# Last layer: the relative scores laid out with the heads innermost, and moved in two halves of 64 rows

## What is computed

```python
attn_scores = jnp.einsum('bhtd,bhsd->bhts', q, k)
rng = jnp.arange(Tx)
rel_pos = jnp.clip(rng[None, :] - rng[:, None], -MAX_REL, MAX_REL) + MAX_REL
rel_emb = rel_pos_emb[rel_pos]
rel_scores = jnp.einsum('bhtd,tsd->bhts', q, rel_emb)
attn = jax.nn.softmax((attn_scores + rel_scores) * scale, axis=-1)
out = jnp.einsum('bhts,bhsd->bhtd', attn, v)
```

## Time and profile before

| | |
|---|---|
| median of 3 runs | 1720.91 us (1717.68 to 1722.53) |
| the profiled execution | 1716.83 us, span 1715.1 us |
| last layer, first and last L707 | 1119.6 and 1656.7 us, 64 tiles |
| L707, one instruction | 1757 ns |
| DVE's wait for `relb` ahead of L707, whole run | 56.7 us |
| DMA share in 1300 to 1600 us | 0.85 |
| mean granted clock | 0.957 |

### The profile page before, as it was taken

How to read it: one execution, slowest core, us unless ns; L and a number is a source line. 1 busy time by engine, 2 the same in 40 slices (tenths; PEclk the granted TensorE clock), 3 DMA queues, 4 the chain that set the end, 5 groups by cost and what they waited for, 6 DMA issues and landing times. The chain is left out here.

```text
span 1715.1 us, 58930 instructions
## 1 busy us (share of the span) xinstructions
PE 1576.5 (92%) x18950; PEld 1439.4 (84%) x18950; DVE 1268.9 (74%) x2908; ACT 1124.7 (66%) x3086; POOL 806.8 (47%) x1457
## 2 busy tenths in 40 slices
PE   3999999999288999999999999679999999999987
PEld 2888888887278999999999999568888888888873
DVE  5899999997784555555555555378899889989876
ACT  2899999998193333433334333288899999999961
POOL 4576667663003222232322322356677776777620
PEclk9999999999598999999999999788999999999987
DMA  4122222222117988888889899286788888888844
GB/s 127 46 73 72 70 70 70 71 72 51 35 37 203 262 252 261 256 256 257 253 258 247 266 257 248 77 220 183 213 227 230 228 223 219 223 222 227 220 117 148
DMA packets 350388, 302.17 MB, mean 176 GB/s; under 512 B 44637, under 2 KB 315442, under 8 KB 350322
## 3 DMA queue, kind: packets, MB, share of 16 engines
q1 hardware_dynamic: 329984, 261.37, 54.5%
q0 software_dynamic: 16032, 37.51, 8.7%
q10 hardware_dynamic: 4306, 2.44, 0.6%
HBM read 208.17 MB, written 93.05 MB: 176 GB/s over the span
## 5 line engine op out<-in xcount | busy, mean ns | idle before, releaser
L1077 ACT ACTIVATE prob<-ps_s,b1s 128x256 f32<-128x256 f32 x426 | 178.8, 471 | 345.3 <-PE ps_s L1044 307.0
L972 POOL DMA_INDIRECT xs<-zn_d,idx x71 | 68.7, 968 | 366.5 <-PE ps_t L1008 364.9
L1044 PE MATMUL ps_s<-xhi,w1hi_c 128*128 128x256 f32 x852 | 236.2, 295 | 1.6 <-ACT xhi L1070 1.6
L1044 PE MATMUL ps_s<-xhi,w1lo_c 128*128 128x256 f32 x852 | 227.1, 284 | 0.0
L1019 PE MATMUL ps_v<-probT,prob 128*128 128x192 f32 x852 | 208.4, 326 | 0.0
L1019 PE MATMUL ps_k<-probT,prob 128*128 128x192 f32 x852 | 208.2, 326 | 0.0
L408 PE MATMUL ps_q<-xT,wqk_c 128*128 128x128 f32 x1536 | 202.8, 284 | 2.2 <-ACT xT L640 2.2
L408 PEld LDWEIGHTS ps_q<-xT,wqk_c 128*128 128x128 f32 x1536 | 194.4, 200 | 5.3 <-ACT xT L640 3.1
L619 ACT ACTIVATE kT<-ps_q,halves 128x128 f32<-128x128 f32 (+1 forms) x512 | 173.0, 366 | 4.9
L1044 PEld LDWEIGHTS ps_s<-xhi,w1hi_c 128*128 128x128 f32 x852 | 164.5, 193 | 2.0 <-ACT xhi L1070 2.0
L1044 PEld LDWEIGHTS ps_s<-xhi,w1lo_c 128*128 128x128 f32 x852 | 164.4, 193 | 0.0
(11 more groups left out here) (225 smaller groups left out, 4180.1 us busy)
## 6 DMA issues: line engine op xcount, KB each, us to landing
rel_d<-rpad SPq DMA_DIRECT2D x64, 864.0 KB
relb<-rel_d SPq DMA_DIRECT2D x64, 768.0 KB, 5.1
probT<-w2h SPq DMA_DIRECT2D x71, 576.0 KB
score<-w1h SPq DMA_DIRECT2D x71, 384.0 KB, 3.4
score<-w1h SPq DMA_DIRECT2D x142, 192.0 KB, 4.5
ys_d<-ys SPq DMA_DIRECT2D x71, 192.0 KB
tok<-b2h SPq DMA_DIRECT2D x71, 96.0 KB
posb<-pos_w SPq DMA_DIRECT2D x128, 48.0 KB, 2.6
```

Of the source, the lines that this page charges most:

```text
L972: pool.indirect_dma_start(xs[b][:, s, :], None, zn_d, bass.IndirectOffsetOnAxis(ap=ix[b][:], axis=0)).then_inc(x_ld[b], 16)
L1044: last = pe.matmul(dst, w, x, start=(k == 0), stop=(k == len(terms) - 1))
L1077: last = act.activation(hT[b][:, c, :], ps_s[:, j, (c % 2) * BLK:(c % 2) * BLK + BLK], ACT.Gelu, bias=b1s[b][:, c:c + 1])
```

## The change

The free dimension of `rpad`, `rel_d` and `relb` is turned from (head, column) to (column, head). So a row of `rel_d` is one contiguous piece, and so is what is stored and loaded of it. The shift of a row is now 12 elements. Store and load are cut in two, rows 0 to 63 and 64 to 127. Rows 0 to 63 need only the columns from 64 on (960 elements of 1728) in the store, and have non-zero values only for keys up to 79 (960 elements of 1536) in the load; the rest of `relb` is set to zero once, by POOL, before its first gathers. ACT reads PSUM in the new order, and DVE reads `relb` with a step of 12 elements from key to key.

```diff
-                        after(act, M[l]["rst"][b], 16 * st.pair("r"))
-                        src = ps_r_in.rearrange("p g (a j) -> p g a j", a=A)
-                        dst = rpad[b][:].rearrange("p (g a) j -> p g a j", g=G)
-                        act.activation(dst[:, :, :, 0:LPAD], src[:, :, :, 0:1].to_broadcast([128, G, A, LPAD]),
-                                       ACT.Copy)
-                        act.activation(dst[:, :, :, LPAD:LPAD + REL], src, ACT.Copy).then_inc(S["r_sb"], 1)
+                        after(act, M[l]["rst"][b], 32 * st.pair("r"))
+                        src = ps_r_in.rearrange("p g (a j) -> p j g a", a=A)
+                        dst = rpad[b][:].rearrange("p j (g a) -> p j g a", g=G)
+                        act.activation(dst[:, 0:LPAD], src[:, 0:1].to_broadcast([128, LPAD, G, A]), ACT.Copy)
+                        act.activation(dst[:, LPAD:LPAD + REL], src, ACT.Copy).then_inc(S["r_sb"], 1)
...
-                        dve.wait_ge(M_["rld"][b], 16 * (st.pair("s") + 1))
-                        dve.tensor_tensor(sc, psv, relb[b][:].rearrange("p (g a) k -> p g a k", g=G),
+                        dve.wait_ge(M_["rld"][b], 32 * (st.pair("s") + 1))
+                        dve.tensor_tensor(sc, psv, relb[b][:].rearrange("p k (g a) -> p g a k", g=G),
                                           ALU.add).then_inc(S["s_rd"], 1)
...
-        rpad = two("rpad", [128, H, LPAD + REL])
-        relb = two("relb", [128, H, B])
+        rpad = two("rpad", [128, LPAD + REL, H])
+        HALVES = [(0, B // 2), (B // 2, B)]
+        relb = two("relb", [128, B, H])
...
-                        heads = rel_d[b][:, 0:HEADW * H].rearrange("t (h c) -> t h c", h=H)
-                        sp.dma_start(heads[:, :, 0:LPAD + REL], rpad[b][:]).then_inc(M_["rst"][b], 16)
-
-                        sp.wait_ge(M_["rst"][b], 16 * (st.pair("r") + 1))
+                        for r0, r1 in HALVES:
+                            c = slice((B - r1) * H, (LPAD + REL) * H)
+                            sp.dma_start(rel_d[b][r0:r1, c], rpad[b][:].rearrange("p j h -> p (j h)")[r0:r1, c])\
+                                .then_inc(M_["rst"][b], 16)
+
+                        sp.wait_ge(M_["rst"][b], 32 * (st.pair("r") + 1))
...
-                        w = ROWW - 1
-                        src = rel_d[b].rearrange("t w -> (t w)")[B - 1:B - 1 + B * w].rearrange("(t w) -> t w", w=w)
-                        src = src[:, 0:HEADW * H].rearrange("t (h c) -> t h c", h=H)[:, :, 0:B]
-                        sp.dma_start(relb[b][:], src).then_inc(M_["rld"][b], 16)
+                        w = ROWW - H
+                        src = rel_d[b].rearrange("t w -> (t w)")[(B - 1) * H:(B - 1) * H + B * w]
+                        src = src.rearrange("(t w) -> t w", w=w)
+                        for r0, r1 in HALVES:
+                            c = slice(0, min(B, r1 + MAXREL) * H)
+                            sp.dma_start(relb[b][:].rearrange("p k h -> p (k h)")[r0:r1, c], src[r0:r1, c])\
+                                .then_inc(M_["rld"][b], 16)
...
             def _(pool):
+                for p in range(2):
+                    pool.memset(relb[p][0:B // 2, B // 2 + MAXREL:B, :], 0.0).then_inc(rel_zero, 1)
                 pool.wait_ge(E_["posi2"], 2)
```

More of the change, by code:

```diff
@@ L1339, in _ @@
             for p in range(2):
-                act.dma_start(rel_d[p][:, 0:HEADW * H].rearrange("t (h c) -> t h c", h=H)[:, :, LPAD + REL:2 * B - 1],
-                              zrow[:].rearrange("p (h c) -> p h c", h=H)).then_inc(rel_zero, 16)
+                act.dma_start(rel_d[p][:, (LPAD + REL) * H:(2 * B - 1) * H], zrow[:]).then_inc(rel_zero, 16)
             output_columns(act, 0)
@@ L1395, in tower @@
         E_ = {"posi2": sem("E_posi2")}
-        rpad = two("rpad", [128, H, LPAD + REL])
-        relb = two("relb", [128, H, B])
+        rpad = two("rpad", [128, LPAD + REL, H])
+        HALVES = [(0, B // 2), (B // 2, B)]
+        relb = two("relb", [128, B, H])
         def in_tiles(buf, width):
-            return buf[:].rearrange("p h s -> p (h s)")[:, 0:NT * width].rearrange("p (t n) -> p t n", n=width)
+            return buf[:].rearrange("p s h -> p (s h)")[:, 0:NT * width].rearrange("p (t n) -> p t n", n=width)
         fg, fr = in_tiles(relb[1], NODES), in_tiles(rpad[0], NODES)
@@ L1404, in tower @@
         prod = in_tiles(relb[0], LEAVES)
-        cT4 = [relb[0][:].rearrange("p h s -> p (h s)")[:, 1024 + 128 * p:1152 + 128 * p] for p in range(2)]
+        cT4 = [relb[0][:].rearrange("p s h -> p (s h)")[:, 1024 + 128 * p:1152 + 128 * p] for p in range(2)]
         fc = sb("fc", [128, NT, 32])
@@ L1419, in decode_pool @@
             if n == 67:
-                pool.wait_ge(M[1]["rst"][0], 16 * (NT // 2))
+                pool.wait_ge(M[1]["rst"][0], 32 * (NT // 2))
                 pool.memset(fr, 1.0).then_inc(F_["fr"], 1)
@@ L1528, in _ @@
                 S, M_ = L[1], M[1]
-                sp.wait_ge(rel_zero, 32)
+                sp.wait_ge(rel_zero, 34)
                 def body(st):
@@ L1535, in body @@
                         settle(sp, spare)
-                        after(sp, M_["rld"][b], 16 * st.pair("r"))
+                        after(sp, M_["rld"][b], 32 * st.pair("r"))
                         settle(sp, spare)
-                        heads = rel_d[b][:, 0:HEADW * H].rearrange("t (h c) -> t h c", h=H)
-                        sp.dma_start(heads[:, :, 0:LPAD + REL], rpad[b][:]).then_inc(M_["rst"][b], 16)
-                        sp.wait_ge(M_["rst"][b], 16 * (st.pair("r") + 1))
+                        for r0, r1 in HALVES:
[3 more added lines that the diff above has]
+                        sp.wait_ge(M_["rst"][b], 32 * (st.pair("r") + 1))
                         settle(sp, spare)
```

## The result

The changed kernel takes 1732.41 us (median of 7 runs, 1726.3 to 1736.29) against 1720.91 us of the kernel before (7 runs, 1717.07 to 1724.69), a ratio of 1.0065 with a 95% interval of 1.0048 to 1.0082: slower, by 11.5 us. The forecast was 1788 us. Direction and bound were right, the size was not: +67 us were forecast.

A forecast was written before the change was run, and what follows sets the result against it. The store-landing-load-store ring bounded the kernel at 8.33 us per tile; DVE would take over. At 9.5 us, 53 tiles add 62 us, early tiles 8, the start 0.5: 1788 us forecast, range 1730 to 1835.

The forecast's parts named there:

- The present bound: Steady tiles before the change: store, landing, load and next store set 8.33 us per tile, no engine does.
- the ring: SP's cycle of store, landing, load and next store of a tile, said to set 8.33 us per tile.
- DMA bytes and the shorter ring: Stores and loads: 1.33 MB for 1.67 in longer pieces, so the cycle falls to 6.1 to 7.2 us, below all engines.
- ACT reads PSUM freely: ACT, L631 and L633: reading PSUM in the new order costs nothing; upper bound 1.4 us more per tile.
- DVE, L707: Stepped read of `relb`: 3.35 us, 1.6 us more per tile, making DVE the bound at 9.14 us.
- PE waits, and its clock falls: PE at L490: about 1.4 us of waiting per tile brings clock falls, taking the tile from 9.14 to 9.5 us.
- The early tiles: The ten tiles ahead of the steady ones: half the DVE price each, +8 us.
- POOL's memsets: Two memsets ahead of the first gather, about 0.55 us each, half hidden: 0.5 us on the path, once.
- 1: Rival: DVE's step costs nothing and the shorter transfers pay, 7.85 us per tile, 1688 us; chance 0.18.
- 2: Rival: 64-row transfers move slower, deciding below some 245 GB/s; at 209 GB/s 9.2 us per tile, 1765 us; chance 0.04.
- 3: Rival: ACT's PSUM reads cost double, DVE's reads nothing; ACT needs 9.25 us per tile, 1765 us; chance 0.03.
- 4: Rival: half-size prices cancel the faster transfers, L707 at some 2.5 us, 1717 to 1726 us; chance 0.03.

The follow-up runs named there:

- e7_flat_whole: The changed kernel with one store and one load of all 128 rows, and DVE reading `relb` in the order in which it lies: 1684.11 us, ratio 0.9802.
- e3_whole: The changed kernel without the halves, one store and one load of all 128 rows a tile: 1719.41 us, ratio to before 1.0024.
- e12: The changed kernel with two stores and two loads a tile, each of all 128 rows and half of the columns: 1720.51 us, ratio 1.0014.
- e6: The kernel before, its layout and flat DVE read kept, with the changed kernel's halves and widths: 1722.25 us, ratio 1.0013.
- e9: A kernel of its own, timing stepped DVE additions, ScalarE copies, loads and stores one at a time; DVE's addition takes 1757 ns at step 1.
- e10: The changed kernel with an added DVE operation on 832 scratch elements ahead of L706 in each tile: 1761.51 us, ratio 1.0249.
- e8: The changed kernel with an added DVE operation on 416 scratch elements ahead of L706 in each tile: 1742.36 us, ratio 1.0126.
- e2: The kernel before, its transfers kept, with DVE's L707 reading `relb` at a step of 12 elements: 1745.98 us, ratio 1.0177.
- e1: The changed kernel with DVE's L706 reading `relb` in the order in which it lies: 1699.97 us, ratio to before 0.9891.

## Why the prediction was right or wrong

**The present bound: right in the main.** e7_flat_whole, with shorter transfers and without DVE's price, falls from 8.33 to 7.91 us a tile, and then PE is full; its need was put at 7.74. But SP's stores and loads were not all of the ring. In the steady stretch of before SP waited for ACT's next rows too:

```profile
SPq L142 <- ACT rpad L633: 48.3, 36, 2.4
```

That is 1.3 us a tile, so SP's own part took 7.0 of the 8.33 us. The rest went by ACT's rows, which come behind L490, and so behind L707.

**DMA bytes and the shorter ring: right in the result, wrong in the reason.** SP's part was forecast at 6.1 to 7.2 us, counted down from 8.33, and it set nothing, as forecast. By the reading just made it was 7.0 us before and is 6.1 in after, but 4.5 in e3_whole and 5.0 in e12. So the longer pieces shortened it and the halves gave more than half of that back. The step that took 311 to 418 GB/s for the halves failed: they moved at 245 GB/s while busy, where before's whole transfers, by the same measure (60.17 MB in 74.5%), moved at 269 and e3's at 353. The stretch of the expert stage that was to bear this out doesn't say how one transfer of 64 rows fares. The width is worth nothing (e6), and the halves cost 7 to 13 us (e3, e12), by a way that the prediction did not look at: in part as waits for the gathers queued beside them.

**ACT reads PSUM freely: right,** 1279 ns for 1278, and 1450 ns for each form alone in e9.

**DVE, L707: the mechanism right, the size off.** 3.35 us were taken from bounds of 2.7 to 3.5; it measured 2.88, 1.78 ns an element. With that the prediction's own sum gives 7.54 + 1.13 = 8.67 us a tile, measured 8.71. Twice the flat price was a round number, not a row; the lower slope (1.66 ns) was the nearer. DVE gets 1.13 us more per tile in place of 1.6, so the term is 0.47 x 53 = 25 us too large. "Writes with a step look free" failed too: in e9 a stepped result costs DVE what a stepped operand does.

**PE waits, and its clock falls: this step failed,** and it was to bring 9.14 up to 9.5 us. PE did wait at L490, 16.0 us on the matmuls, but its busy time was 8.2 us a tile, so it idled 0.5 us a tile and not 1.4, and the clock was 1.00. The 1.4 us came from the need of 7.74 us, for which the waits of PEld were taken off PE's time; PE itself was busy for 293.59 of 300 us, so it had idled 0.18 us a tile and not 0.59. e10 puts the 9.15 us there: PE idles 0.8 us a tile, the clock is 0.98, the time 1761.5 us. The row behind the fear has 1.48 us idle in 3.40. PE's longest wait at L490 in the steady stretch is 0.9 us in after and in e8, where the clock held. Yet in e10, whose gaps ahead of one fall were 0.80 us each, the 6.7 us behind them (1331.50 to 1338.20 us) have a granted clock of 0.50, and e2 has 0.98 in that stretch. So falls can come behind short gaps as well, but they were few; what decides whether one comes stays open.

**The early tiles: sign wrong.** +8 us were forecast, -7 measured, since the falls that before had there did not come. How much of that is chance is not known: e3, e10 and e12 had 0.93 in 1150 to 1200 us, e8 0.83.

**POOL's memsets: hidden.** L706 starts 1.7 us sooner than before, as the first block ran 2.0 us sooner.

The sum was made against the profiled execution, so it is compared with that of after, 1726.3 us: 1787 - 1726 = 61 us too much. 25 by the price, 19 (0.36 x 53) by the clock and 15 in the early tiles are 59; start and end (3.5) and the memsets (0.5) add 4, and the 0.04 us by which 8.71 exceeds 8.67 take 2 back. The low end of the stated range, 1730 us, was built from L707 at 2.7 us and no fall of the clock, and that is nearly what came.

**The rivals.** 1 fell with L706 at 2884 ns; e1 shows that it would have given 1700 us with these halves, not 1688. 2 was right about the halves' rate, 245 GB/s at its own threshold, and wrong in making it the bound. By the Trainium skill's page "SBUF — State Buffer", "Door 1: The DMA port swizzle", 64 rows reach half of the ports, at most 218 GB/s. e9's lone half agrees in kind, since it lands about as late as twice its bytes; its rate by the busy share, 236 GB/s, is a little above the page's figure, and the measurement decides. 3 fell. 4 was off by its price.

## What to carry to other kernels

Before interleaving a layout for longer DMA pieces, price the engine that reads it: put the stepped read alone into the old kernel. Interleave in small groups so that elements stay near each other, and let the PSUM side take the large step. Don't save bytes by sending 64 rows at a time: whole transfers of 128 rows with a quarter more bytes were 13 to 22 us faster by the times and 7 to 24 by the ratios, in part because what was queued beside them landed sooner.

## What was not expected of the hardware

- The price of a step in SBUF is not by its size but in stairs: 1757 ns at 4 and 8 B, 2182 at 12, 2857 at 16, 2816 at 48. The Trainium skill's page "SBUF — State Buffer", "Door 1: The DMA port swizzle", speaks of lines of 16 B that need two hits each for the full rate. The stairs agree, with two elements a line free at 8 B, and one at 16 B costing 1.76 ns an element. 96 B (3932 ns) lies outside that rule and stays open.
- ScalarE pays it as well, reading or writing SBUF: 2868 and 2822 ns at a step of 12 against 1482 and 1450 flat. With PSUM as the stepped source (3 and 12 elements) both engines pay nothing.
- A load of the upper 64 rows lands about as late as one of 128 rows with twice the bytes (4.2 and 4.3 us).
